# Second cross-attention of a fused layer: products in column halves, one piece behind each score, and the key split moved off VectorE

## The reference, cut to what matters

```python
def _L1_xattn_ref(qkv, y):              # qkv [4, 512, 512], y [4, 512, 1601]
    q = qkv.reshape(bs * 16, 32, length)
    k = v = y.reshape(bs * 16, 32, -1)
    scale = 1.0 / math.sqrt(math.sqrt(ch))
    weight = jnp.einsum('bct,bcs->bts', q * scale, k * scale)
    weight = jax.nn.softmax(weight.astype(jnp.float32), axis=-1)
    return jnp.einsum('bts,bcs->bct', weight, v)
...
x = x + jnp.tanh(g_xattn[1]) * _L1_xattn_ref(_layernorm(x, axis=-1), ctx_2048)
```

## Time and profile before

| | |
|---|---|
| runs | median 1873.78 us (1870.95 to 1878.46) |
| the profiled execution | 1874.35 us, its span 1872.5 us |
| stage C in the span | about 702 to 1597 us |
| busy over the span | PE 86%, DVE 66%, ACT 43%, POOL 43% |
| mean granted TensorE clock | 0.947 of full speed |

### The profile page before, as it was taken

One profiled execution on the slowest core, in us unless ns is written; L12 is line 12 of the kernel. 1 busy time (PEld: TensorE's weight loads), 2 busy tenths in 40 slices (PEclk: granted clock), 3 DMA queues, 4 the chain that ended last, 5 costly groups with the idle time before them and its releaser, 6 DMA issues. The chain is left out here.

```text
span 1872.5 us, 22112 instructions
## 1 busy us (share of the span) xinstructions
PE 1619.3 (86%) x7540; PEld 635.7 (34%) x7568; DVE 1240.2 (66%) x1554; ACT 808.1 (43%) x1225; POOL 799.9 (43%) x308
## 2 busy tenths in 40 slices
PE   5999999799677886898888888888888887699898
PEld 2444444344333441222222222222222221344443
DVE  3768999885456558787777777777777740444443
ACT  1321211221443431666666666766666666111110
POOL 0022233543211124666677787676667777000000
PEclk9999999899899995999999999999999999799999
DMA  9232223212211113222211222222212142000000
GB/s 329 71 111 75 82 84 102 82 57 106 68 34 34 26 32 112 72 74 73 74 47 52 63 61 74 75 74 74 61 44 62 44 90 49 1 10 14 22 22 23
DMA packets 136395, 124.36 MB, mean 66 GB/s; under 512 B 61774, under 2 KB 112226, under 8 KB 136294
## 3 DMA queue, kind: packets, MB, share of 16 engines
q1 hardware_dynamic: 131302, 112.56, 21.5%
q10 hardware_dynamic: 4992, 10.49, 1.7%
HBM read 73.49 MB, written 10.76 MB: 45 GB/s over the span
## 5 line engine op out<-in xcount | busy, mean ns | idle before, releaser
L1474 ACT ACTIVATE c_prob<-c_scores,ctx_scales 128x512 f32<-128x512 f32 (+1 forms) x832 | 520.1, 684 | 271.3 <-PE c_scores L1530 265.9
L1374 DVE TENSOR_REDUCE c_piece_max<-c_unit 128x1 f32<-128x804 f32 x512 | 485.4, 984 | 194.3 <-PE c_unit L1513 189.8
L1315 POOL TENSOR_TENSOR c_prob_sum<-c_prob_sum,c_prob 128x2048 f32<-128x2048 f32 x96 | 436.6, 4548 | 16.1 <-ACT c_prob L1474 9.8
L1530 PE MATMUL c_scores<-c_queries,c_keys 97*128 97x512 f16 (+1 forms) x832 | 316.6, 394 | 64.6 <-ACT c_prob L1474 57.3
L1513 PE MATMUL c_unit<-c_khigh,c_qdiag 128*128 128x402 f16 x1024 | 277.0, 354 | 55.1 <-DVE c_piece_max L1374 44.0
L1539 PE MATMUL c_out<-c_prob,c_VT 128*32 128x512 f32 (+1 forms) x1664 | 225.5, 622 | 0.0
L676 PE MATMUL a_S<-a_ctxT,a_xnT 128*128 128x401 f32 x512 | 192.6, 521 | 7.2 <-ACT a_prob L633 3.9
L706 PE MATMUL a_o<-a_ctx,a_probT 128*128 128x512 f32 (+1 forms) x416 | 183.5, 598 | 0.0
L1530 PEld LDWEIGHTS c_scores<-c_queries,c_keys 97*128 97x128 f16 (+1 forms) x832 | 80.0, 99 | 301.9 <-ACT c_prob L1474 232.0
L1513 PEld LDWEIGHTS c_unit<-c_khigh,c_qdiag 128*128 128x128 f16 x1024 | 87.0, 100 | 232.1 <-DVE c_piece_max L1374 131.3
L1315 POOL TENSOR_TENSOR c_prob_sum<-c_prob 128x2048 f32<-128x2048 f32 x16 | 72.6, 4538 | 191.8 <-ACT c_prob L1474 191.8
(11 more groups left out here) (196 smaller groups left out, 1924.3 us busy)
## 6 DMA issues: line engine op xcount, KB each, us to landing
c_k<-in_keys SPq DMA_DIRECT2D x16, 801.0 KB, 6.9
c_keys<-c_khigh SPq DMA_DIRECT2D x128, 100.1 KB, 2.2
a_ctx<-in_ctx SPq DMA_DIRECT2D x12, 1024.0 KB, 6.0
c_VT<-in_values SPq DMA_DIRECT2D x16, 768.0 KB
a_ctxT<-in_ctxT SPq DMA_DIRECT2D x12, 802.0 KB, 4.7
c_keys<-c_krest SPq DMA_DIRECT2D x64, 100.1 KB, 2.2
a_weights<-in_L_ffn_weight SPq DMA_DIRECT2D x3, 1408.0 KB, 14.3
weights_back<-a_weights SPq DMA_DIRECT2D x3, 1408.0 KB, 9.0
```

The costliest lines, as they stand in the source:

```text
L1315: nc.gpsimd.tensor_tensor(psum4[:], a[:], prob[(j * MC + c) % RING][:], ALU.add).then_inc(sums_taken, 2 if i == 1 else 1)
L1374: nc.vector.tensor_reduce(piece_max[j % 2][:, k // 2, k % 2:k % 2 + 1], U[bank(unit)][:, :, 0:PIECE], axis=AX.XY, op=ALU.max).then_inc(uni ...
L1474: nc.scalar.activation(prob[(j * MC + c) % RING][0:w, h, :], STp[h % 2][0:w, :], ACT.Exp, scale=score_scale[0:w]).then_inc(exp_done, 1)
L1530: nc.tensor.matmul(STp[h % 2][0:w, :], K[p][:, h, c * P:c * P + w], Q[p][:, h, :], start=True, stop=True).then_inc(scores_ready, 1)
```

## The change

The values products and denominator products are split into column halves (256 of 512 queries), except chunk 0's values and chunk 4's denominator. `placed` gives each piece a place: gap 4c + h is what PE does behind score h of chunk c, and 52 to 55 are the gaps behind the next group's chunk 0. At most gaps one piece stands. The last chunk's denominator and `den_of_sum` move into gaps 4 to 7 of the next group's slot. Units are placed where a running sum of weights (0.53 per half, 0.36 per unit) is behind its even course, and the rows unit not before gap 42. Followed, the 36 pieces' gaps are 4 to 7, 9, 12 to 15, 17, 19, 21, 22, 23, 25, 27, 29, 31, 33 to 37, 39, 41, 43, 45 to 54, and the units fall: 0 in gap 6, 1 and 2 in gap 8, 3 and 4 in 11, 5 in 14, 6 and 7 in 16, then to 16 in gap 29, 26 in gap 42, 30 in gap 51, and the last two in gap 55.

The key split changes: ACT scales the keys in place (f32) and then copies them to f16, and GpSimd subtracts for the rest, as the last work of its slot. DVE's reciprocals stand before units 3 to 6, and `take_out` before the first exponential of chunk 1.

```diff
@@ gpsimd
+            def rest_of_k(n, j):
+                pool.wait_ge(khigh_ready, n + 1)
+                wait(pool, stacked, (n - 1) * STACKS)
+                nc.gpsimd.tensor_tensor(krest[j][:], kt[j][:], khigh[j][:], ALU.subtract).then_inc(krest_ready, 1)
...
                 add_up(g, j, 7)
                 if more:
                     rest_of_q(g + 2, j % 2)
+                    rest_of_k(g + 2, j % 2)
@@ vector
-            def rest_of_k(n, j):
-                dve.wait_ge(khigh_ready, n + 1)
-                wait(dve, stacked, (n - 1) * STACKS)
-                nc.vector.scalar_tensor_tensor(krest[j][:], kt[j][:], key_scale, khigh[j][:], ALU.mult, ALU.subtract).then_inc(krest_ready, 1)
...
-                    if before and u % 2 == 0 and u // 2 < PARTS:
-                        finish(g - 1, u // 2)
+                    if before and 3 <= u < 3 + PARTS:
+                        finish(g - 1, u - 3)
...
-                    if main and more and unit[2:] == (j + 2, 6):
-                        rest_of_k(g + 2, j % 2)
@@ scalar
-                nc.scalar.activation(khigh[j][:], kt[j][:], ACT.Copy, scale=key_scale).then_inc(khigh_ready, 1)
+                nc.scalar.activation(kt[j][:], kt[j][:], ACT.Copy, scale=key_scale).then_inc(kscaled, 1)
+                act.wait_ge(kscaled, n + 1)
+                nc.scalar.copy(khigh[j][:], kt[j][:]).then_inc(khigh_ready, 1)
...
-                act.wait_ge(pv_done, PV0 + (g + 1) * CHUNKS)
+                act.wait_ge(out_done, g + 1)
...
-                    if c == 0 and h == 2 and (not isinstance(g, int) or g > 0):
+                    if c == 1 and h == 0 and (not isinstance(g, int) or g > 0):
                         take_out(g - 1)
@@ tensor
+            def columns(half):
+                return slice(0, D) if half == WHOLE else slice(half * D // 2, (half + 1) * D // 2)
...
+                    last = nc.tensor.matmul(O[h * CH:(h + 1) * CH, cols], VT[j % 2][0:w, c, h * CH:(h + 1) * CH],
+                                            prob[(j * MC + c) % RING][0:w, h, cols], start=c == 0, stop=c == MC - 1 and half == 1)
...
+            def placed(before):
+
+                gaps = {}
+                for c in range(1, MC):
+                    for b in {1: [], 2: [0], 3: [1, 2]}.get(c, [c - 1]):
+                        at = 4 * c + (1 if b == c - 1 else 0)
+                        if b == 0:
+                            gaps.setdefault(at + 1, []).append(("out", b, WHOLE))
+                            continue
+                        gaps.setdefault(at, []).append(("out", b, 0))
+                        gaps.setdefault(at + (2 if b not in SUMMED else 1), []).append(("out", b, 1))
+                        if b == SUMMED[0]:
+                            gaps.setdefault(at + 2, []).append(("den", b, WHOLE))
+                        elif b in SUMMED:
+                            gaps.setdefault(at + 2, []).append(("den", b, 0))
+                            gaps.setdefault(at + 3, []).append(("den", b, 1))
+                for half in range(2):
+                    gaps.setdefault(4 * MC + 1 + half, []).append(("out", MC - 1, half))
+                if before:
+                    for i in range(4):
+                        gaps.setdefault(4 + i, []).append(("last", None, i))
+                return gaps
...
+                    upto = (gap - 3) * per_gap
+                    while given < len(stream) and (done + PAIR / 2 <= upto or gap == 4 * MC + 3):
...
+                for c in range(1, MC + 1):
                     for h in range(H):
+                        if c < MC:
+                            score(g, j, c, h)
+                        elif nxt:
+                            score(g + 1, j + 1, 0, h)
+                        products(4 * c + h)
```

More of the change, by code:

```diff
@@ L1319, in _ @@
             rest_of_q(0, 0)
+            rest_of_k(0, 0)
             steps.link(pool.memset(QZ[1][:], 0.0))
@@ L1322, in _ @@
             rest_of_q(1, 1)
+            rest_of_k(1, 1)
             steps.link(pool.memset(ones32[:], 1.0))
@@ L1530, in score, with out @@
                 nc.tensor.matmul(STp[h % 2][0:w, :], K[p][:, h, c * P:c * P + w], Q[p][:, h, :], start=True, stop=True).then_inc(scores_ready, 1)
-            def out(g, j, c):
-                w = P if c < MC - 1 else ML
+            WHOLE = 2
+            def columns(half):
+                return slice(0, D) if half == WHOLE else slice(half * D // 2, (half + 1) * D // 2)
+            def out(g, j, c, half):
+                w, cols = P if c < MC - 1 else ML, columns(half)
                 if c == 0:
@@ L1536, in out, with den @@
                     wait(pe, out_taken, g)
-                pe.wait_ge(exp_done, EXPS0 + g * EXPS + H * (c + 1))
+                if half != 1:
+                    pe.wait_ge(exp_done, EXPS0 + g * EXPS + H * (c + 1))
                 for h in range(H):
-                    last = nc.tensor.matmul(O[h * CH:(h + 1) * CH, :], VT[j % 2][0:w, c, h * CH:(h + 1) * CH],
-                                            prob[(j * MC + c) % RING][0:w, h, :], start=c == 0, stop=c == MC - 1)
-                return last
-            def den(g, j, c):
-                k = ML if c == MC - 1 else P
+                    last = nc.tensor.matmul(O[h * CH:(h + 1) * CH, cols], VT[j % 2][0:w, c, h * CH:(h + 1) * CH],
+                                            prob[(j * MC + c) % RING][0:w, h, cols], start=c == 0, stop=c == MC - 1 and half == 1)
+                if half > 0:
+                    if c == MC - 1:
+                        last.then_inc(out_done, 1)
+                    elif c not in SUMMED:
+                        last.then_inc(pv_done, 1)
+            def den(g, j, c, half):
+                w, cols = P if c < MC - 1 else ML, columns(half)
                 if c == SUMMED[0]:
@@ L1558, in out_and_den, with den_of_sum @@
-            def out_and_den(g, j, c):
-                last = out(g, j, c)
-                if c in SUMMED:
-                    last = den(g, j, c)
-                last.then_inc(pv_done, 1)
+                if half > 0:
+                    last.then_inc(pv_done, 1)
+            def den_of_sum(g, half):
+                cols = columns(half)
+                if half == 0:
+                    pe.wait_ge(sums_taken, (g + 1) * NP)
+                for h in range(H):
+                    last = nc.tensor.matmul(DEN[h * CH:(h + 1) * CH, cols], ones32[:], psum4[:, h, cols], start=False, stop=half == 1)
+                if half == 1:
+                    last.then_inc(den_done, 1)
@@ L1572, in slot, with products @@
                     return
-                first_gap, gaps = 0, H * MC
-                per_gap = max(len(stream), UNITS) / (gaps - first_gap)
-                gap = given = 0
-                def units():
-                    nonlocal gap, given
-                    gap += 1
-                    upto = round((gap - first_gap) * per_gap)
-                    while given < min(len(stream), upto):
+                before = not isinstance(g, int) or g > 0
+                gaps = placed(before)
+                HALF, PAIR = 0.53, 0.36
+                weights = {gap: sum(HALF * (1 + (what != "last" and half == WHOLE)) for what, b, half in parts) for gap, parts in gaps.items()}
+                per_gap = (sum(weights.values()) + PAIR * max(len(stream), UNITS)) / (H * MC)
+                given, done = 0, 0.0
+                def products(gap):
+                    nonlocal given, done
+                    for what, b, half in gaps.get(gap, []):
+                        if what == "out":
+                            out(g, j, b, half)
+                        elif what == "den":
+                            den(g, j, b, half)
+                        else:
+                            last_sums(g - 1, (j - 1) % TURN, half)
+                        done += HALF * (1 + (what != "last" and half == WHOLE))
+                    upto = (gap - 3) * per_gap
+                    while given < len(stream) and (done + PAIR / 2 <= upto or gap == 4 * MC + 3):
                         unit = stream[given]
-                        if unit[0] == "rows" and upto <= AHEAD + ROWS_AT:
+                        if unit[0] == "rows" and gap < ROWS_GAP:
                             break
@@ L1586, in units @@
                         given += 1
[L1588 to L1589 removed]
+                        done += PAIR
+                ROWS_GAP = 4 + round((AHEAD + ROWS_AT) * H * MC / UNITS)
+                for c in range(1, MC + 1):
                     for h in range(H):
[L1591 to L1609 removed]
+                        if c < MC:
[3 more added lines that the diff above has]
+                        products(4 * c + h)
+                if not nxt:
+                    for i in range(4):
+                        last_sums(g, j, i)
                 assert given == len(stream), (given, len(stream))
```

37 lines of the change are left out of this document (8 added, 29 removed).

## The result

The changed kernel takes 1893.05 us (median of 4 runs, 1892.8 to 1893.35), the kernel before 1873.5 us in the runs beside it: a ratio of 1.0101, 95% interval 1.008 to 1.0122. It is slower, by 19.5 us; the forecast was 1862 us, faster. The profiled execution took 1892.8 us with a span of 1891.0, so the sum of 1862 is compared with a time 31 us above it.

The account below looks back on a forecast made before the run. PE was taken as the carrier, its waits setting the period. 13 groups at 52.5 instead of 53.0 us give -6.5, group 14 -1.0, the last -5.1: -12.6 from 1874.35, so 1862 us; range 1828 to 1884.

Parts of the forecast that it names:

- the two accounts: Set up before the follow-up runs: PE's order (24 more blocks, late DVE, branch) decides; or the new hole and lower clock.
- The block price: PE entering and leaving a block of products between scores: 0.24 us beside the products, possible range 0.10 to 0.34.
- the half product at half a whole's time: PE's product on 256 columns: taken as half of a whole product's 0.86 us.
- the hole in chunk 3: PE, done with gap 13 at 9.7 us, stands 2.4 us while ACT makes two key passes; gap 14 starts at 12.1.
- the late gain: GpSimd's gain waits for DVE's fourth reciprocal, ending at 15.45 us; its next addition starts at 18.2 instead of 12.1.
- the exponential held by an addition: Chunk 7's first exponential waits for GpSimd's addition of chunk 3, in at 27.5 us; PE starts score 30 at 28.2.
- 24 x 0.24: PE's work per group: 36 blocks instead of 12 raise it from 42.1 to 47.8 us.
- Then gaps 30 to 51 are ... 20.4: PE from score 30 to score 52: scores, pairs, half products and blocks at their prices take 20.4 us; period 52.2.
- I charge 0.3 on average: Lower clock behind gap 13's hole: costs up to 1.7 us, 1.3 in hand against GpSimd; 0.3 charged, 52.5 us per group.
- The ends: Groups outside the regular 13: group 0 set to 0, group 14 -1.0 us, last group -5.1, prologue 0.
- No change: Rival: lower clock behind the new hole delays unit 5 and GpSimd's chain; 53.2 us per group, 1871 us; chance 0.17.
- Slower: Rival: half products' weight loads aren't hidden, each block costs 0.10 us more; 54.8 us per group, 1896 us; chance 0.15.

Follow-up runs that it names:

- after_single: The changed kernel with at most one unit placed in a gap, behind a score: 1861.53 us, ratio 0.9934 to the kernel before.
- after_recips: The changed kernel with DVE's four reciprocals before units 1 to 4 instead of 3 to 6: 1885.21 us, ratio 1.0069 to the kernel before.
- after_late: The changed kernel with ACT's f32 scaling of the keys moved behind chunk 7's exponentials, one pass after chunk 2: 1860.16 us, ratio 0.9921 to the kernel before.
- after_adjacent: The changed kernel with both halves of each product in one gap, 19 blocks instead of 36: 1884.85 us, ratio 1.0058 to the kernel before.

## Why the prediction was wrong

The forecast was faster, by 12.6 us; measured is slower by 1%, and 31 us above the forecast. The range (1828 to 1884) did not reach it. Each of the two accounts holds in part: spreading the units takes off 32 us, halving the hole 33, writing out the loop 13, and the halves are not cheap, with 50 us on top of the keys' part.

**Sizes that held.** The block price, the half product at half a whole's time, the place and length of the hole in chunk 3, GpSimd's time for the keys' rest (3.2 for 3.6), the late gain, the exponential held by an addition, and the length of the last group (47.9 for 46.5) came near what was worked out. So did the sign of the keys' part. With the keys done alike, the halves raise the typical period from 50.28 to 54.46. The step "24 x 0.24", 5.8 us of PE's work, was in the sum; how much of the 4.2 us it makes is not shown, since 1.3 of them come with the clock and PE's waits changed too.

**First failed step: "Then gaps 30 to 51 are ... 20.4".** PE's waits for DVE's maxima were set to zero there. The trace of before had shown a unit's maximum at about 1 us, so a pair every 0.345 us in one gap must wait once its buffers are full; I counted units and didn't follow the buffers. In group 10, where the clock is undisturbed, score 28 comes at 24.9 (forecast 25.1) and score 30 at 27.8 (28.2), but gap 32 takes 1.22 for 0.91, gap 42 1.96 for 1.26 and gap 44 1.25 for 0.91, and gaps 30 to 51 in all 21.8 for 20.4. The period is 53.13 where 52.2 was foreseen. after_single takes these waits away where the clock doesn't fall, and lands at 51.89.

Behind this stands a path that the sum didn't have. From the pair in gap 25 to those in gap 32 DVE works with no pause above 0.2 us; its run begins so in group 9 and in group 10:

```profile
1278.19 3.70 DVE L1384 TENSOR_REDUCE c_piece_max<-c_unit 128x1 f32<-128x804 f32 x4 [2.66 <-PE c_unit L1516]
```

```profile
1331.15 3.87 DVE L1384 TENSOR_REDUCE c_piece_max<-c_unit 128x1 f32<-128x804 f32 x4 [2.66 <-PE c_unit L1516]
```

That is T + 24.6 and T + 23.1, and score 33 comes 7.2 and 7.3 us later (31.80 and 30.46). The sum had GpSimd's additions as what PE waits for in this stretch. In after_recips ACT doesn't wait for them, and score 33 of group 9 still starts at 31.80.

**Second: "I charge 0.3 on average" for the lower clock.** The clock fell behind the hole in nine of the 11 regular groups, and between neighbours it cost 1.3 us (54.46 in group 9, 53.13 in group 10). The argument was that PE has 1.3 us in hand against GpSimd. That was so: score 30 starts at 28.19 in group 9, with the clock fallen, and at 27.77 in group 10. But DVE's run from gap 25 on had been delayed by 1.5 us too, and the loss came out at gap 32, 2.16 instead of 1.22 us. A reserve against one chain is none against another. after_late, with half the hole, has no fall behind it in any of these groups, and a period of 51.84. Together the two steps make 595.0 us in the 11 regular groups instead of 577.5: +17.5.

**Third: no term for the loop's branch.** Groups 7 and 8 took 115.8 us against 105 forecast, +10.8, of which 6.9 are above two regular groups of the kernel after (2 x 54.46). The loop's body had grown with the products' matmuls, and the trace of before, where these two groups stood only 1.2 us above two regular ones, had nothing in it that I read as a warning. It did hold one: PE stands 1.28 us at this place, and the two groups are 2.0 and 1.2 us longer than others with the same clock. Written out, the two groups are regular.

**The ends** make the rest: group 0 +0.8, group 14 +1.1 and the last +1.4 against their terms. 17.5 + 10.8 + 3.3 = 31.6, of 31 us.

**The rivals.** "No change" had the lower clock as its cause, at about half its size, but sent the delay through GpSimd's chain; after_recips shows that it doesn't come that way. "Slower" had nearly the number (1896) by a mechanism that after_adjacent rules out, since halves' weight loads cost nothing: its nearness is luck. The part of the forecast whose price I had doubted most, the block, was exact, and those that I had set to nothing or nearly made the result. What the range lacked was a case in which two such terms fail together.

**What stays open.** Why a hole of about the same length brings the lower clock in one group and not in the next. That PE waits for code at the branch is argued, not shown: the four instruction packets stand at the branch of the kernel before too, and no run changed the size of the loop by itself. What the runs show is that the stand goes with the branch.

## What to carry to other kernels

Before spreading work over finer pieces, price each change of tile shape on TensorE between two unlike neighbours, here 0.24 us, and count how many the new order has; before crediting a gap with it, follow the buffers of every engine that is fed there, not the sum of the work. A reserve that hides a delay has to be in hand on every chain that the delay touches. Of a change with several parts run each alone: here one part gained 1.7% and, with its pass placed where no one waits for it, 2.8%, while the whole was 1% slower.

## What the runs showed of the hardware that was not expected

- Two matmuls of 256 columns cost as much as one of 512 in the same tile shape: a block of 16 takes 1.07 us, one of 8 whole ones 1.06.
- At the one branch back of the loop PE stood 2.63 us and ACT 2.52 for nothing that the profile shows, and a stretch of 6.8 us at the lower clock followed at 1195.3; the one at 1209.0 stands behind the group's usual hole. Groups 7 and 8 take 7 us more than two typical ones in the kernel after and 1 us more in the kernel before, whose loop has the same number of turns; beside groups with the same clock it is 3 us there.
- Nearly the same hole of PE (2.6 and 2.4 us) is followed by the lower clock in 10 groups of the kernel before and in 4 when only its loop is written out, worth 1.5 to 2.0 us per group. In the kernel after, written out, it still follows in 10 groups. A stand of 0.5 us there (after_late, gap 13) is followed by it in none.
- DVE's rest of the keys and GpSimd's operations slow each other: the rest takes 1.89 us alone and 4.56 beside an addition, and GpSimd's addition on one column went from 1.78 to 0.19 us when that operation left DVE. DVE's maxima aren't touched: they take 0.93 to 1.00 us each, with and without an addition beside them.
